# Other places for the first five and the last four of 32 elements in a hand-ordered decoder kernel, and ten fewer filler products

## The chip, the cores and the metric

The kernel runs on one core of a Trainium2 chip. Its time is the device time in microseconds (us) of that core, from the first to the last instruction and what lies around them. It holds one launch with 32 independent batch elements. The engines are TensorE (PE), VectorE (DVE), ScalarE (ACT), GpSimd (POOL) and SyncE (SP, which here only issues DMAs).

## The reference

Four layers are applied to `x` (32 elements of 128 tokens by 256 features) with a context of the same shape. Cut to what matters:

```
# layer 0: attention of x with the context; only element 0's result is used, and is added to all
return tgt + att[0]
# layer 1: a Mamba block, then cross attention with 8 heads
zxbcdt = rms(x, norm_w) @ in_proj_w;  z, xBC, dt = split(zxbcdt);  dt = softplus(dt + dt_bias)
xBC = silu(conv_b + sum(padded[:, k:k+L] * conv_w[:, k] for k in range(4)))
h = h * exp(dt * A) + (dt * xh) B^T;  y = h C            # a scan over the 128 tokens, 8 heads
x = x + rms((y + D_skip * xh) * silu(z)) @ out_proj_w
x = x + softmax(masked(ln(x) Wq (enc Wk)^T / sqrt(dh))) (enc Wv) @ Wo
# layer 2: causal self attention, layernorm, cross attention, layernorm, relu feed-forward, layernorm
# layer 3: causal cross attention, layernorm, gelu feed-forward (256 -> 1024 -> 256), residual
```

## The kernel before

An element passes through some 93 tasks, each with a name: `x1` (x plus layer 0's result), `x1r` and `xhat` (its normalised input), `xhatT`, `z0`, `z1`, `xbc0`, `xbc1` (input projections), `dt`, `softplus`, `am`, `ld` (the step widths and the decay rates, a long chain of small operations on POOL), `spread` (the rates sent to all 128 partitions through DRAM), `conv0`, `conv1`, `silu`, `pairs`, `scan`, `decayed`, `Y` (the Mamba block), `uT`, `proj`, `xnT`, `Q1`, `K1`, `V1`, `quads1`, `scores1`, `turn1`, `values1`, `finish1`, `ctxT`, `Wo` (the first attention) and so on to `up0`, `up1`, `down`, `store`. The attentions 2, 3 and 4 have `quads` (scores), `mT` (row maxima turned), `quadsT` (scores turned), `exps`, `values`, `attT`, `back`, `finish` and `norm`. `x1.1` below is task `x1` of element 1, the second one; elements are counted from 0. One task can have parts on several engines: `V4` is a product on PE, an addition on DVE and a memset on POOL.

The order of the tasks on every engine is fixed when the kernel is built. Each task has a due time in `TASKS`; element n stands 14 units after element n-1. The first eight elements are moved by the numbers in `FIRST`, the last six by those in `LAST`, tasks that are done once stand at `SETUP`, and `SHIFT` moves a task on one engine against PE:

```
moved = FIRST.get(task, ...)[n] if n < FEW_FIRST else LAST.get(task, ...)[n - B] if n >= B - FEW_LAST else 0
return round(TASKS[task] + PERIOD * n + moved, 4)
```

Every engine then runs its tasks strictly in that order, and waits at each for what it needs. So does the queue of SP: a transfer is issued only when all that stand before it have been. The results of products go to four PSUM banks that are used in turn (`job`, L282): a product waits until the job four places before it in PE's order has been read out.

In places where PE is expected to wait, `spare` (L630) has it multiply the identity matrix with itself a given number of times; the results are never read. `SPARE` gives the counts for the start (113 in all), `SPARE_LAST` those for the last element (36):

```
for _ in range(times):
    mm(t[:, 0:P], ident, ident, start=True, stop=True)
```

The loads of all weights are issued at the start by SP in the order `load_mamba`, `load_w1`, `load_w2`, and then `loadx.1`, the input of element 1. `load_w3` (five transfers, 2.75 MB) comes later. `x1` needs its element's input to have landed:

```
dve.wait_ge(S[f"x_in{l % 2}"], nth_of_two(it, l) * 16)
```

Of the kernel before, what the change touches and what calls it, by code (L numbers as in the profile page):

```python
# [54 lines left out]
    finish2=43.1974, finish3=49.378, finish4=63.2585, ld=21.3616, loadc=21.5812, loadx=-12.121, mT2=40.0837, mT3=48.4859,
    mT4=58.9877, n2=40.7882, n3=47.7104, norm2=33.7236, norm3=22.9718, norm4=37.5768, norm5=62.8256, pairs=21.8762, proj=26.9634,
    quads1=31.0824, quads2=38.3064, quads3=46.4563, quads4=57.4583, quadsT2=40.7773, quadsT3=49.6848, quadsT4=61.9224, row=44.5976,
    scan=14.2492, scores1=32.2004, scores2=32.0011, scores3=47.3368, scores4=68.1586, silu=20.9204, softplus=18.9875,
# [1647 lines left out]
```

## Time and profile before

| what | us |
|---|---|
| median of 3 runs (1661.57 to 1665.08) | 1662.71 |
| the profiled execution | 1660.65 |
| its span, first to last instruction | 1658.9 |
| PE busy in it | 1610.9 |
| DVE busy in it | 1387.6 |
| ACT busy in it | 1075.2 |
| POOL busy in it | 499.7 |

The profile is of one execution, 2.06 us shorter than the median. Busy times include the filler products. A row of the timeline gives the start in us from the span's start, the busy time, engine, line, operation, what is written and read, the shapes and the count; in brackets the idle time just before it and what ended it. A float32 product of the program is two records on PE, so 9 filler products are x18 there.

### The profile page before, as it was taken

To read this page: it belongs to the slowest core of one execution; us is meant where nothing else is said; L and a number is where in the kernel's file an instruction comes from. 1 tells how busy PE (TensorE), PEld (TensorE's weight loads), DVE (VectorE), ACT (ScalarE), POOL (GpSimd) and SP (SyncE) were. 2 spreads that over 40 slices of the span, in tenths; PEclk is the share of its full clock that TensorE was granted. 3 is DMA by queue.
4 is the path that set the end of the run, shared out by engine and by line. 5 is a ranking of instruction groups with operands and counts; after the bars stand their busy time and mean duration, and the time that the engine had idled before them with its cause. 6 is when DMAs were issued, how large, how long until landed. Compare 5 with 4: busy or idle time off the path is not lost.

```text
span 1658.9 us, 61223 instructions
## 1 busy us (share of the span) xinstructions
PE 1610.9 (97%) x25035; PEld 1386.5 (84%) x25035; DVE 1387.6 (84%) x3587; ACT 1075.2 (65%) x2798; POOL 499.7 (30%) x1256
## 2 busy tenths in 40 slices
PE   7899999999999999999999999999999999999987
PEld 6778888888888888888888888888888888888776
DVE  4688888888888889888889888888988888898662
ACT  2356766776666676666667676667766666766663
POOL 2333223333322332332233232233333223323110
PEclk9999999999999999999999999999999999999999
DMA  6210001000000000000000000000000000000000
GB/s 224 76 36 24 3 18 31 18 24 28 22 3 24 25 25 25 25 23 4 25 25 25 25 25 7 20 24 25 25 25 25 2 25 25 22 28 19 5 5 8
DMA packets 31317, 44.38 MB, mean 27 GB/s; under 512 B 3008, under 2 KB 26176, under 8 KB 30912
## 3 DMA queue, kind: packets, MB, share of 16 engines
q1 hardware_dynamic: 30496, 39.93, 7.6%
q8 instruction: 202, 3.31, 0.9%
q14 instruction: 75, 0.61, 0.1%
q10 hardware_dynamic: 544, 0.52, 0.1%
HBM read 36.12 MB, written 4.33 MB: 24 GB/s over the span
## 4 chain that ended last, share of the span: by engine, by line
PE 54%; DVE 36%; issue 4%; POOL 3%; DMA 1%; ACT 1%; DVEq 0%; SPq 0%; POOLq 0%; ACTq 0%
PE ring L639 19%; PE ring L645 14%; PE ring L627 5%; DVE conv L1371 5%; DVE maxima_at L1269 5%; PE score L707 4%; DVE decay L1405 4%; PE score L731 2%; PE ring L773 2%; DVE conv L1377 2%; DVE decay L1409 2%; PE ring L860 2%; DVE QB L1280 2%; DVE bn L1239 2%; DVE conv L1366 2%
## 5 line engine op out<-in xcount | busy, mean ns | idle before, releaser
L1546 POOL TENSOR_TENSOR stat<-stat 128x1 f32<-128x1 f32 x224 | 132.0, 596 | 603.3 <-DVE stat L1235 602.8
L1026 ACT COPY actT<-ring 128x256 f32<-128x256 f32 x256 | 95.6, 374 | 259.0 <-PE ring L627 258.7
L1269 DVE TENSOR_REDUCE maxima_at<-score 128x4 f32<-128x512 f32 x388 | 240.8, 684 | 21.0 <-PE score L707 19.8
L1059 ACT ACTIVATE weights<-score 128x512 f32<-128x512 f32 x388 | 200.6, 606 | 28.1 <-PE score L731 27.6
L1371 DVE SCALAR_TENSOR_TENSOR conv<-raw,vectors,conv 128x128 f32<-128x128 f32 x576 | 168.5, 348 | 6.8
L639 PE MATMUL ring<-actT,w_q 128*128 128x128 f32 x1024 | 141.5, 281 | 0.7 <-ACT actT L1026 0.7
L639 PEld LDWEIGHTS ring<-actT,w_q 128*128 128x128 f32 x1024 | 124.5, 191 | 12.8 <-issue 11.3
L639 PE MATMUL ring<-actT,w_up 128*128 128x128 f32 x1024 | 127.6, 278 | 0.5 <-ACT actT L1026 0.5
L639 PEld LDWEIGHTS ring<-actT,w_up 128*128 128x128 f32 x1024 | 119.1, 192 | 3.5 <-ACT actT L1026 1.0
L1195 ACT ACTIVATE gT<-ring,vectors 128x128 f32<-128x128 f32 x256 | 73.2, 369 | 68.7 <-PE ring L639 68.0
L645 PE MATMUL ring<-w_down,gT 128*128 128x256 f32 x512 | 115.9, 379 | 1.3 <-issue 1.3
L731 PE MATMUL score<-QB,KE 32*128 32x128 f32 x3104 | 114.8, 284 | 1.0 <-DVE QB L1280 1.0
L731 PEld LDWEIGHTS score<-QB,KE 32*128 32x128 f32 x3104 | 96.2, 187 | 19.9 <-issue 15.4
L773 PE MATMUL ring<-weights,V 128*32 128x128 f32 x3104 | 104.9, 276 | 1.6 <-issue 1.3
L1077 ACT ACTIVATE KE<-K,const 128x128 f32<-128x128 f32 x256 | 106.3, 503 | 0.0
L645 PEld LDWEIGHTS ring<-w_down,gT 128*128 128x128 f32 x512 | 94.9, 190 | 13.1 <-issue 1.4
L639 PE MATMUL ring<-cT,w_k 128*128 128x128 f32 x768 | 104.4, 279 | 0.0
L1070 ACT COPY attT<-ring 128x512 f32<-128x512 f32 x97 | 56.3, 580 | 71.0 <-PE ring L773 70.8
L645 PE MATMUL ring<-w_v,cT 128*128 128x256 f32 x384 | 100.6, 385 | 0.5 <-ACT V L1043 0.5
L639 PEld LDWEIGHTS ring<-cT,w_k 128*128 128x128 f32 x768 | 95.4, 192 | 4.9 <-issue 0.2
L1280 DVE SCALAR_TENSOR_TENSOR QB<-ring,const,QB 128x256 f32<-128x256 f32 x194 | 84.4, 476 | 17.7 <-PE ring L627 17.6
L773 PEld LDWEIGHTS ring<-weights,V 128*32 128x32 f32 x3104 | 79.1, 109 | 23.5 <-ACT V L1043 11.8
(180 smaller groups left out, 3843.9 us busy)
## 6 DMA issues: line engine op xcount, KB each, us to landing
decay<-rates_out SPq DMA_DIRECT2D x32, 512.0 KB, 4.1
cT<-in_ctxT SPq DMA_DIRECT2D x32, 128.0 KB, 2.2
x_in<-in_x SPq DMA_DIRECT2D x32, 128.0 KB, 2.5
out<-result SPq DMA_DIRECT2D x32, 128.0 KB, 2.1
row_all<-in_rows SPq DMA_DIRECT2D x1, 1420.0 KB, 10.2
w_in<-in_in_proj SPq DMA_DIRECT2D x1, 1288.0 KB, 6.9
w_k<-in_k SPq DMA_DIRECT2D x4, 256.0 KB, 8.6
w_v<-in_v SPq DMA_DIRECT2D x4, 256.0 KB, 7.6
```

The lines of the kernel that those rows point to most:

```text
L627: last = nc.tensor.transpose(t[:, c * P:(c + 1) * P], src[:, c * P:(c + 1) * P], ident)
L639: last = mm(t[:, at:at + P], w[:, c, cols:cols + P], xT[:, c, :], start=(c == 0), stop=(c == n - 1))
L645: last = mm(t[:, at:at + hi - lo], xT[:, c, :], w[:, c, lo:hi], start=(c == 0), stop=(c == n - 1))
L731: last = mm(score[:, r, at:at + P], KE[rows_of, l, c, e, :], QB[rows_of, l, c, e, :], start=(not masked and at == 0), stop=(c == DC - 1 an ...
L773: last = mm(output[ROWS_OF[r], four * P:(four + 1) * P], V2[:, l, h, :], weights[:, buffer, h % 8 // 2, at:at + P], start=True, stop=True)
L1026: nc.scalar.copy(dst.rearrange("p c k -> p (c k)"), t[:, 0:n]).then_inc(read, 1)
L1059: run(weights[:, turned_buffer(it, a_, l), r, :], score[:, r, :], ACT.Exp).then_inc(S["exps"], 1)
L1077: last = run(KE[:, l, c, e, :], K2[:, l, c, :], ACT.Identity, scale=own[:, e:e + 1], bias=spare_row[:, 2 * c + e:2 * c + e + 1])
L1269: nc.vector.tensor_reduce(maxima_at[:, maxima_buffer(it, a_, l), 32 * r:32 * (r + 1)].rearrange("p (f s) -> p s f", f=2)[:, 0:DC, :], scor ...
L1280: last = stt(QB[:, l, :, e, :], t[:, 0:P].unsqueeze(1).broadcast_to((P, DC, P)), either_row[:, e:e + 1], QB[:, l, :, e, :], ALU.mult, ALU.add)
L1371: last = stt(conv[:, l % 2, c, :], raw[:, l % 2, c, k:k + P], conv_w[:, c, k:k + 1], conv[:, l % 2, c, :], ALU.mult, ALU.add)
L1546: tt(stat[:, l, 10:11], stat[:, l, 2:3], stat[:, l, 4:5], ALU.pow).then_inc(S[done], 1)
```

## The change

`TASKS`, `SHIFT` and `SPARE_LAST` have the same numbers as before. New are the entries of elements 0 to 4 in `FIRST` and of elements 28 to 31 in `LAST` (all 93 tasks of each), all of `SETUP`, and 9 of the 15 counts in `SPARE`. No instruction is added or taken away but filler products: 103 in place of 113. Elements 5 to 27 keep their due times, and PE runs the same order as before from `fc2.5` to `values1.25`. Two of the changed table lines, and the counts:

```
-    x1=(-5.3355, -6.7716, -12.2611, 0.5214, 0.2413, 0.0991, 0, 0.8625),
+    x1=(-5.017, -12.3112, -7.2487, 0.1142, 1.8596, 0.0991, 0, 0.8625),
...
-SPARE = {("mT0", 0): 11, ("values0", 0): 9, ("back0", 0): 3, ("xhatT", 0): 6, ("ld", 0): 16, ("pairs", 0): 5, ("Y", 0): 18, ("uT", 0): 6, ("xnT", 0): 9, ("ctxT", 0): 10, ("x2T", 0): 7, ("Y", 1): 3, ("mT2", 0): 4, ("back2", 0): 3, ("n3", 0): 3}
+SPARE = {("mT0", 0): 11, ("values0", 0): 9, ("back0", 0): 3, ("xhatT", 0): 13, ("ld", 0): 16, ("pairs", 0): 5, ("Y", 0): 14, ("uT", 0): 6, ("xnT", 0): 6, ("ctxT", 0): 7, ("x2T", 0): 4, ("Y", 1): 2, ("mT2", 0): 3, ("back2", 0): 3, ("n3", 0): 1}
```

The new tables stand on more lines, so every line behind them has a number that is higher by 22.

**DVE, around the first use of element 1's input.** Before, behind element 0's normalised input (`att<-res,stat`) come the preparations of constants, `q1_bias` to `k4_bias` and on to the weights, and only after both convolutions `res<-x_in,att0`, which is `x1.1`:

```order
L1307 TENSOR_SCALAR att<-res,stat 128x256
L1333 TENSOR_SCALAR q1_bias<-ring2 128x1
L1333 TENSOR_SCALAR q1_bias<-ring3 128x1
...
L1371 SCALAR_TENSOR_TENSOR conv<-raw,vectors,conv 128x128 x9
L1299 TENSOR_TENSOR res<-x_in,att0 128x256
L1377 SCALAR_TENSOR_TENSOR conv<-raw,conv 128x768
L1393 TENSOR_TENSOR state_gate<-ring3,const 128x128
L1397 TENSOR_TENSOR dbx<-ring0,dts 128x512
L1399 TENSOR_TENSOR dx<-ring0,row_all 128x512
L1235 TENSOR_SCALAR stat<-stat 128x1
L1405 SCALAR_TENSOR_TENSOR decay<-decay,delta 128x1024
```

Of the change, from the same instruction on (L1329 is the L1307 above):

```order
L1329 TENSOR_SCALAR att<-res,stat 128x256
L1321 TENSOR_TENSOR res<-x_in,att0 128x256
L1355 TENSOR_SCALAR q1_bias<-ring3 128x1
L1355 TENSOR_SCALAR q1_bias<-ring0 128x1
...
L1399 SCALAR_TENSOR_TENSOR conv<-raw,conv 128x768
L1374 TENSOR_SCALAR w_q1<-w_q1,vectors 128x256 x2
L1329 TENSOR_SCALAR att<-res,stat 128x256
L1415 TENSOR_TENSOR state_gate<-ring3,const 128x128
L1419 TENSOR_TENSOR dbx<-ring0,dts 128x512
L1421 TENSOR_TENSOR dx<-ring0,row_all 128x512
L1427 SCALAR_TENSOR_TENSOR decay<-decay,delta 128x1024
```

`x1.1` moved from behind the convolutions to the place ahead of the preparations, and `xhat.1` (the second L1329) stands ahead of element 0's `pairs` and `scan`; before it stood behind element 0's `xnT`.

**SP, from the first `spread` on.** `decay<-rates_out` is `spread`, `rates_out<-rates_row` is `ld`; the five rows from `w_q` to `w_down` are `load_w3`. Before:

```order
L582 DMA decay<-rates_out 128x1024
L578 DMA rates_out<-rates_row 8x128
L573 DMA cT<-in_ctxT 128x2x128
L561 DMA x_in<-in_x 128x256
L582 DMA decay<-rates_out 128x1024
L555 DMA w_q<-in_q 128x2x256
L555 DMA w_k<-in_k 128x2x256
L555 DMA w_v<-in_v 128x2x256
L555 DMA w_up<-in_up 128x2x1024
L555 DMA w_down<-in_down 128x8x256
```

Of the change:

```order
L604 DMA decay<-rates_out 128x1024
L577 DMA w_q<-in_q 128x2x256
L577 DMA w_k<-in_k 128x2x256
L577 DMA w_v<-in_v 128x2x256
L577 DMA w_up<-in_up 128x2x1024
L577 DMA w_down<-in_down 128x8x256
L600 DMA rates_out<-rates_row 8x128
L595 DMA cT<-in_ctxT 128x2x128
L604 DMA decay<-rates_out 128x1024
```

`load_w3` follows element 0's `spread` directly; before it followed element 1's.

**PE, the last element's last attention.** `w_v4,cT` is `V4.31`, `w_fc2` is `fc2.31`, `QB,KE` is `quadsT4.31`, `ring2<-const` are nine filler products, `weights,V2` is `values4.31`. Before:

```order
L639 MATMUL ring3<-actT,w_fc1 128x128 x4
L645 MATMUL ring0<-w_v4,cT 128x256 x2
L645 MATMUL ring1<-w_fc2,fc1T 128x256 x2
...
L731 MATMUL score<-QB,KE 128x128 x16
L634 MATMUL ring2<-const 128x128 x9
L773 MATMUL ring2<-weights,V2 32x128 x16
```

Of the change:

```order
L661 MATMUL ring3<-actT,w_fc1 128x128 x4
L667 MATMUL ring0<-w_fc2,fc1T 128x256 x2
...
L753 MATMUL score<-QB,KE 128x128 x16
L667 MATMUL ring1<-w_v4,cT 128x256 x2
L656 MATMUL ring2<-const 128x128 x9
L795 MATMUL ring2<-weights,V2 32x128 x16
```

`V4.31` moved from between `fc1.31` and `fc2.31` to the place between `quadsT4.31` and the fillers.

## Rows read from the trace of the kernel before

**Rows 1.** The page's first part: busy us, share of the span, instructions
```profile
PE 1610.9 (97%) x25035; PEld 1386.5 (84%) x25035; DVE 1387.6 (84%) x3587; ACT 1075.2 (65%) x2798; POOL 499.7 (30%) x1256
```

**Rows 2.** Windows: stretch, length, busy us by engine, granted TensorE clock, DMA share, GB/s
```profile
0.00:80.00 80.00, 64.35 (x681) 57.52 (x685) 44.40 (x125) 24.88 (x70) 24.63 (x62) 0.98 0.43 141
80.00:160.00 80.00, 74.17 (x1235) 61.14 (x1234) 69.68 (x182) 47.30 (x126) 27.36 (x70) 1.00 0.13 41
160.00:1540.00 1380.00, 1369.54 (x21746) 1182.52 (x21739) 1214.78 (x3132) 942.36 (x2459) 433.87 (x1096) 1.00 0.07 21
1600.00:1660.00 60.00, 47.55 (x547) 40.10 (x547) 19.83 (x50) 23.24 (x53) 5.13 (x11) 0.93 0.02 6
```

**Rows 3.** Timeline of DVE, element 0: `xhat`, the last preparation, `softplus`
```profile
24.05 0.35 DVE L1307 TENSOR_SCALAR att<-res,stat 128x256 f32<-128x256 f32 x1 [0.85 <-POOL stat L1546]
...
26.01 0.45 DVE L1342 TENSOR_SCALAR k_bias<-vectors,const 128x1 f32<-128x1 f32 x2
...
29.32 0.17 DVE L1385 TENSOR_SCALAR dts<-dts 128x8 f32<-128x8 f32 x1 [1.28 <-ACT dts L1110]
```

**Rows 4.** The line that loads inputs (L561), 21 to 23 us: `loadx.1`
```profile
L561 SPq DMA_DIRECT2D x_in<-in_x x1: 1077/1077/1077, 21.8 to 21.8; - x1
...
DMA to landing us min/median/max: 7.1/7.1/7.1
```

**Rows 5.** Timelines of POOL (`softplus.0` begins) and PE (`ld.0`)
```profile
30.11 0.20 POOL L1571 TENSOR_TENSOR dts<-dts 128x8 f32<-128x8 f32 x1 [1.06 <-DVE dts L1387]
...
36.15 0.27 PE L851 MATMUL ring<-const,dts 128*8 128x128 f32 x1 [3.37 <-POOL dts L1591]
```

**Rows 6.** The line of `spread` (L582), for element 0 and element 1
```profile
L582 SPq DMA_DIRECT2D decay<-rates_out x1: 430/430/430, 38.1 to 38.1; - x1
DMA to landing us min/median/max: 4.0/4.0/4.0
...
L582 SPq DMA_DIRECT2D decay<-rates_out x1: 430/430/430, 73.0 to 73.0; - x1
...
DMA to landing us min/median/max: 5.2/5.2/5.2
```

**Rows 7.** Timeline: both scans, element 0's first attention, element 1's chain between them
```profile
42.94 2.28 DVE L1405 TENSOR_TENSOR_SCAN decay<-decay,delta 128x1024 f32<-128x1024 f32 x1
...
59.84 1.29 DVE L1260 TENSOR_REDUCE neg_max<-score 128x4 f32<-128x512 f32 x2 [3.67 <-PE score L687]
...
64.99 0.17 DVE L1387 TENSOR_TENSOR dts<-dts 128x8 f32<-128x8 f32 x1
65.54 0.76 PE L750 MATMUL ring<-V,weights 128*32 128x33 f32 x64 [1.04 <-ACT weights L1064]
...
65.96 2.70 DVE L1371 SCALAR_TENSOR_TENSOR conv<-raw,vectors,conv 128x128 f32<-128x128 f32 x9
...
68.82 0.42 DVE L1440 TENSOR_TENSOR att<-ring,rec 128x256 f32<-128x256 f32 x1
...
71.08 0.27 PE L851 MATMUL ring<-const,dts 128*8 128x128 f32 x1 [0.48 <-POOL dts L1591]
...
78.18 2.29 DVE L1405 TENSOR_TENSOR_SCAN decay<-decay,delta 128x1024 f32<-128x1024 f32 x1 [1.04 <-DMA decay<-rates_out]
```

**Rows 8.** Timeline of DVE: `xnT.1`
```profile
92.08 0.41 DVE L1245 TENSOR_SCALAR att<-res,stat 128x256 f32<-128x256 f32 x1 [0.77 <-POOL stat L1546]
```

**Rows 9.** Timelines of the tail: `scores3.30`, `V4.31`, nine fillers, `values4.31`
```profile
1561.84 2.49 DVE L1269 TENSOR_REDUCE maxima_at<-score 128x4 f32<-128x512 f32 x4 [2.49 <-PE score L707]
...
1621.00 1.03 PE L645 MATMUL ring<-w_v,cT 128*128 128x256 f32 x4
...
1638.10 2.27 PE L634 MATMUL ring<-const 128*128 128x128 f32 x18
1640.35 1.08 PE L773 MATMUL ring<-weights,V 128*32 128x128 f32 x32
```

**Rows 10.** Windows with PE alone: stretch, length, busy, granted clock, DMA
```profile
38.00:40.00 2.00, 2.00 (x9) 0.50 0.79 238
```

More of the change, by code:

```diff
@@ L55 @@
[L55 to L58, printed above, removed]
@@ new lines @@
+    pairs=21.8762, proj=26.9634, quads1=31.0824, quads2=38.3064, quads3=46.4563, quads4=57.4583, quadsT2=40.7773,
+    quadsT3=49.6848, quadsT4=61.9224, row=44.5976, scan=14.2492, scores1=32.2004, scores2=32.0011, scores3=47.3368,
+    scores4=68.1586, silu=20.9204, softplus=18.9875, spread=22.7901, store=23.1605, turn1=32.8102, uT=26.5226, up0=66.8312,
+    up1=67.8745, values1=33.4323, values2=42.004, values3=50.5514, values4=63.0522, x1=14.4949, x1r=12.6782, x2T=35.2831,
+    x3T=44.7168, x4T=52.7176, x5T=55.6828, x6T=65.7536, xbc0=16.7051, xbc1=18.0605, xhat=30.6529, xhatT=15.884, xnT=28.5927,
@@ L194 @@
-        fc1=0.7372, ld=-0.1039, row=0.2044, scores1=-0.7902, silu=-0.1882, softplus=-0.2365, turn1=0.1793, uT=0.4762, up0=0.6797,
-        up1=0.4246, x1=-0.5175, x2T=-0.0673, x3T=0.071, x4T=0.2522, x5T=0.318, x6T=0.3578, xbc0=0.1868, xbc1=0.439, xhatT=0.0635,
-        xnT=0.9282, z0=0.0015, z1=0.2322, K0=-24.9607, Q0=-31.7526, V0=-0.7018, attT0=-21.6729, exps0=39.9731, prep_in=-3.1006),
-    DVE=dict(
-        K1=1.0572, K3=0.57, V4=0.4841, Wo=1.1062, Y=0.609, conv0=3.1201, conv1=22.4343, decayed=-7.3402, down=1.5737, e2=0.5677,
-        e3=-0.0785, fc2=0.652, finish1=43.3665, finish2=0.278, finish3=2.0689, finish4=1.3234, mT2=0.6229, mT3=0.8259, mT4=0.5286,
-        n2=0.9079, n3=0.7485, norm2=10.4211, norm3=29.708, norm4=17.8864, norm5=2.0685, pairs=0.2116, proj=0.8909, scan=10.8396,
-        scores1=-0.5025, scores2=7.84, scores3=-0.7238, scores4=-9.0893, silu=1.0136, softplus=0.4775, uT=0.6437, x1=-1.3524,
-        x1r=1.7364, x3T=0.0339, xhat=-15.2978, xnT=0.2024, finish0=3.4964, mT0=-11.4439, prep_in=10.1597, prep_masks=14.7529,
-        prep_out=12.705, prep_q1=-0.1445, scores0=-43.4431),
+        K0=-24.9607, K2=0.4275, K4=0.371, KE2=2.1051, KE3=-8.3627, Q0=-31.7526, Q1=0.2401, Q2=0.4113, Q3=0.0246, Q4=1.2096,
@@ new lines @@
+        V0=-0.7018, V1=0.0661, V2=0.6553, V3=0.3112, Y=1.0681, attT0=-21.6729, attT2=-3.4331, attT3=31.0217, attT4=8.7138,
+        ctxT=-0.4571, exps0=39.9731, exps2=-6.4438, exps3=39.9244, exps4=40.2808, fc1=0.7372, ld=-0.1039, prep_in=-3.1006,
+        row=0.2044, scores1=-0.7902, silu=-0.1882, softplus=-0.2365, turn1=0.1793, uT=0.4762, up0=0.6797, up1=0.4246,
+        x1=-0.5175, x2T=-0.0673, x3T=0.071, x4T=0.2522, x5T=0.318, x6T=0.3578, xbc0=0.1868, xbc1=0.439, xhatT=0.0635,
+        xnT=0.9282, z0=0.0015, z1=0.2322),
@@ new lines @@
+    DVE=dict(
+        K1=1.0572, K3=0.57, V4=0.4841, Wo=1.1062, Y=0.609, conv0=3.1201, conv1=22.4343, decayed=-7.3402, down=1.5737,
+        e2=0.5677, e3=-0.0785, fc2=0.652, finish0=3.4964, finish1=43.3665, finish2=0.278, finish3=2.0689, finish4=1.3234,
+        mT0=-11.4439, mT2=0.6229, mT3=0.8259, mT4=0.5286, n2=0.9079, n3=0.7485, norm2=10.4211, norm3=29.708, norm4=17.8864,
+        norm5=2.0685, pairs=0.2116, prep_in=10.1597, prep_masks=14.7529, prep_out=12.705, prep_q1=-0.1445, proj=0.8909,
+        scan=10.8396, scores0=-43.4431, scores1=-0.5025, scores2=7.84, scores3=-0.7238, scores4=-9.0893, silu=1.0136,
+        softplus=0.4775, uT=0.6437, x1=-1.3524, x1r=1.7364, x3T=0.0339, xhat=-15.2978, xnT=0.2024),
```

280 lines of the change are left out of this document (149 added, 131 removed).

## The prediction

> **What bounds the kernel now.** I read the busy times first, then the windows. PE is busy for 1610.9 of 1658.9 us [rows 1], so it is the engine to look at; but the windows split the kernel in three [rows 2]. From 160 to 1540 us PE is busy 1369.54 of 1380 us: the middle is PE's own work, and no order of tasks can shorten it by more than the 10.5 us left. In the first 80 us PE is busy 64.35 and DVE 44.40: neither is full, so chains of single operations set the pace there, and much of PE's time is filler: the counts up to `x2T.0` are 100 of the 113. From 80 to 160 us PE is busy 74.17 and DVE 69.68; both are near their limit. In the last 60 us PE is busy 47.55, DVE 19.83: chains again. So the change, which touches the ends alone, can win only what its chains become shorter at the two ends; once PE is full, a shift is handed on unchanged through the middle to the tail, since the same work follows.
>
> Then I read the timelines of both ends for what ended each wait. In the start one chain stands out for each element: the step widths on POOL, `ld` on PE, `spread` by DMA, the scan on DVE. Element 0's scan begins at 42.94, element 1's at 78.18, and the second is released by the DMA [rows 7]. What moves that 78.18 moves what follows.
>
> **The change part by part.**
>
> *Ten fewer fillers.* Nine take 2.27 us [rows 9], so ten are 2.5 us. They cost something only where PE would otherwise be ready earlier; at all the places where the counts fall, PE waits for DVE or ACT behind the fillers anyway. Priced at nothing; what covers it is that wait. Without it the gain would be up to 2.5 us.
>
> *x1.1 ahead of the preparations.* Element 1's input is issued at 21.8 behind all weights and lands 7.1 us later, at 28.9 [rows 4]. DVE is free for it when `xhat.0` ends, 24.05 + 0.35 = 24.40 [rows 3]. DVE takes its tasks in order, so it stands for 4.5 us, and behind it wait the preparations (24.40 to 26.01 + 0.45 = 26.46, 2.1 us [rows 3]) and `softplus.0`. `x1.1` itself has no row here; as a pass over 256 elements like `xhat.0` it is taken as 0.4. `softplus.0` on DVE then begins at 28.9 + 0.4 + 2.1 = 31.4, not 29.32 [rows 3]: 2.1 us late. The move of the weight scalings behind the convolutions doesn't help, since DVE had waited 1.28 before that anyway. PE is touched too: `bias0` now lies in the bank that `xbc1.0` needs, and is read by the first preparation, so `xbc1.0` waits till 29.5; `conv1.0` needs it only at 35, so that costs nothing.
>
> From the start of `softplus.0` on POOL (30.11) to `ld.0` (36.15) are 6.0 us of fixed steps [rows 5], so `ld.0` goes to 38.3. `spread.0` was issued at 38.1 and goes to 40.2. It took 4.0 us, but now `load_w3` is issued right behind it, as it was behind element 1's, and that one took 5.2 [rows 6]. So the rates land at 45.4 with the 5.2, at 44.2 with the 4.0. I take 5.2: it is the row with the same five transfers behind it. The scan of element 0 goes from 42.94 to 45.4, 2.5 us late (bounds 1.3 and 2.5).
>
> Two transfers on one queue start in order, says the Trainium skill (DMA: Bandwidth & Descriptors, Two DMAs through the same engine are not ordered), but are pipelined. By order alone `load_w3` behind could not slow `spread`, the 4.0 would hold, and the sum below would be 1.2 us lower. The 5.2 of element 1 speaks against it, with one row.
>
> *xhat.1 ahead of the first scan.* Element 1's projections now fill PE beside element 0's scan, and its `conv0` stands on DVE ahead of `scores1.0`, where DVE waited 3.67 us [rows 7]; it took 3.5 us there (2.70 in nine passes and 0.85 in three, as `conv1.1` [rows 7]), and fits. `scores1.0` itself follows element 0: 59.84 + 2.5 = 62.3. Behind it, with no convolution between, comes `softplus.1`: 1.3 for the maxima and 0.6 for three small steps give 64.2, where before they ended at 64.99 + 0.17 = 65.16 [rows 7]. That is 1.0 us earlier. The same POOL chain then releases `ld.1` at 71.08 - 1.0 = 70.1; before, it had ended a 0.48 us wait of PE [rows 7], so it was the last. In its way on PE stands `ctxT.0`, which needs `finish1.0`; that had waited for `conv1.1` until 68.8, and now stands ahead of it. `values1.0` ended at 65.54 + 0.76 = 66.30 [rows 7], 6.5 us behind the start of `scores1.0`; in that, ACT did the copies of `z1.1`, `xbc1.1` and `V1.1` between the exponentials and the turned weights, about 1.6 us that the new order puts elsewhere. So `finish1.0` comes at 62.3 + 4.9 = 67.2. `spread.1` goes from 73.0 to 72.0, and, with no `load_w3` behind, takes 4.0 instead of 5.2: it lands at 76.0. Element 1's scan goes from 78.18 to 76.0: **2.2 us earlier**. With `spread.0` at 4.0 as well it would be 3.4. The other way to the scan, `conv1.1` from 67.8 (3.5), its tanh and product (0.9 and 1.0) and `pairs.1` (1.9), ends at about 75.8, just in time. So the late element 0 is forgiven, as long as nothing there takes longer.
>
> *xhat.2 ahead of xnT.1.* It fills 0.35 of a wait of 0.77 on DVE [rows 8] in a stretch where DVE is near full: 0.35 us. Other exchanges between 80 and 500 us have no row of their own; bounded by PE's idle time, (80 - 74.17) in 80 to 160 and about 2 behind it, and below by the same on the other side. I take nothing.
>
> *The tail.* `quads1.31` waited for its bank; `Q3.30` (a product of about 1 us) now stands in that place, and `turn1.31` and its wait no longer stand ahead of `quads3.30`. `scores3.30`, for which DVE waited 2.49 from 1559.35 [rows 9], can begin as soon as some 1560.4 instead of 1561.84, and everything of element 31 up to `Wo` follows it by 1.2 us. Against it, `V4.31` took 1.03 where PE waited for ACT's relu in any case, and now stands in front of nine fillers whose end (1640.37) met the start of `values4.31` at 1640.35 [rows 9]: there was no room, so it costs 1.0. Net -0.2.
>
> Sum: -2.2 - 0.35 - 1.2 + 1.0 = -2.7 us. Against the profiled 1660.65 that is 1657.9. That execution lies 2.06 below the median of 1662.71; moved to the median, **1660.0**.
>
> **The clock.** After PE's wait of 3.37 before `ld.0` [rows 5] the granted clock fell to half, 0.50 in 38 to 40 us [rows 10], which is the 1.2 GHz level; there nine records filled 2 us. In the change PE waits twice, 1.3 before `xbc1.0` and some 2.4 before `ld.0`. If it falls again, V1.0 and five fillers stand twice as long ahead of `pairs.0`, some 1.2 us more; that is inside the wait for the rates. In the tail the clock is 0.93 over the last 60 us [rows 2]; a stretch more or less at half clock moves the end by 1 to 2 us either way.
>
> The Trainium skill (TensorE: Matmul & The Clock Gate, What's actually happening) has activity release the throttle. By that rule fewer fillers are a risk, not a gain: each stretch that falls costs as said above, a sum up to 1.5 us higher. The row after `ld.0`'s wait agrees; no row shows it after a wait under 1 us.
>
> **The rivals.**
> *More is won* (0.34). `spread.0` isn't slowed by `load_w3` (-1.2), PE isn't at half clock near `pairs.0`, and the fuller DVE order of elements 1 to 4 saves a part of the 5.8 us of PE's idle time in 80 to 160 us, some 1.5: 1660.0 - 2.7 = 1657.3. For it: both stretches are near full, so each wait filled counts. Against: DVE, not PE, has the longer queue there.
> *Nothing arrives* (0.16). Element 1's scan comes 2.2 earlier, but PE spends it waiting later, before element 3; the tail is -0.2. 1662.5. For it: the last scans of the start are already at the steady distance. Against: from 92 us on DVE has hardly a wait to lose it in.
> *Slower, the wait for element 1's input* (0.12). The 4.5 us of DVE at `x1.1` aren't forgiven: `finish1.0` now stands ahead of `conv1.1`, and with 75.8 against 76.0 there is no slack. If element 0's attention or `conv1.1` comes later than here worked out, each us goes through. It decides from 2.2 us on; above that, the whole delay of element 0 and the loss of that gain show. An input that lands 4 us later than 28.9, with the queue as full as it is, gives -2.7 + 2.2 + 4 = +3.5: 1666.2.
>
> **How the numbers follow.** My forecast has 0.38, with its own range 1658.4 to 1661.6 (bounds of `spread` and one half-clock stretch). A measurement of this kernel tells 0.2%, 3.3 us, from no change, so faster is below 1659.4. Of the forecast a third lies below, with the first rival 0.34: 0.45. The second rival and the rest of the forecast: 0.42. Slower than 1666.0: 0.13. The range holds the forecast, nearly all of the first two rivals: 1655.2 to 1663.8.
>
> **What would show it.** In the changed kernel DVE waits 4.5 us for the DMA at `x1.1` (L1321) from 24.4; `ld.0` at 38.3; scans at 45.4 and 76.0; `spread.0` 5.2 and `spread.1` 4.0 us to landing; `finish1.0` ahead of `conv1.1` near 67; the middle as far apart as before; in the tail `V4.31` directly before the fillers and `values4.31` at 1.0 more behind `quadsT4.31`. The forecast is wrong if element 1's scan isn't near 76, or if the distance from it to the first full stretch grows.

## The result and the profile after

The change is slower, not faster: 1665.54 us median of 20 executions against 1662.53 of the kernel before, ratio 1.0022, 95% interval 1.0014 to 1.0031. In three later comparisons it stood 8.1, 6.9 and 5.9 us above the kernel before. The forecast was 1660.0, or 2.7 faster.

The page's first part for the changed kernel (compare [rows 1]), and its windows, in the columns of [rows 2]:

```profile
PE 1611.0 (97%) x25015; PEld 1387.0 (83%) x25015; DVE 1391.1 (84%) x3587; ACT 1075.3 (65%) x2798; POOL 494.6 (30%) x1256
```

```profile
0.00:80.00 80.00, 63.31 (x677) 56.98 (x677) 48.43 (x125) 25.71 (x70) 23.00 (x61) 0.96 0.48 161
80.00:160.00 80.00, 72.83 (x1208) 60.03 (x1212) 69.54 (x182) 47.07 (x126) 26.44 (x71) 1.00 0.06 16
160.00:1540.00 1380.00, 1366.42 (x21680) 1180.05 (x21674) 1211.23 (x3126) 941.11 (x2456) 431.49 (x1096) 1.00 0.07 21
```

The third row is the surprise. PE works there at the same full clock, and from 336 to 1363 us it has the same products in the same order as before; still it is busy 1366.42 of 1380 us where it was 1369.54, so it is idle 3.1 us more in a stretch of which the change touches only the two ends. The profiled execution took 1667.32 us, 6.7 more than that of before. When each product of PE is held against the same product of the kernel before, the changed kernel is level at 370 us (0.02 late), 2.3 late at 1363 us and 6.7 late at the end. So about a third of this execution's loss lies in the untouched middle, and two thirds behind it.

The first 80 us went nearly as worked out. DVE's timeline, with `x1.1`'s wait, `softplus.0`'s last step on DVE and both scans (compare [rows 3] and [rows 7]):

```profile
28.51 0.42 DVE L1321 TENSOR_TENSOR res<-x_in,att 128x256 f32<-128x256 f32 x1 [4.42 <-DMA x_in<-in_x]
...
31.35 0.17 DVE L1409 TENSOR_TENSOR dts<-dts 128x8 f32<-128x8 f32 x1
...
45.06 2.28 DVE L1427 TENSOR_TENSOR_SCAN decay<-decay,delta 128x1024 f32<-128x1024 f32 x1
...
67.56 0.42 DVE L1462 TENSOR_TENSOR att<-ring,rec 128x256 f32<-128x256 f32 x1
...
75.72 2.28 DVE L1427 TENSOR_TENSOR_SCAN decay<-decay,delta 128x1024 f32<-128x1024 f32 x1
```

And `ld.0` on PE, then the line of `spread` for elements 0 and 1 (compare [rows 5, 6]):

```profile
37.73 0.27 PE L873 MATMUL ring<-const,dts 128*8 128x128 f32 x1 [2.57 <-POOL dts L1613]
```

```profile
L604 SPq DMA_DIRECT2D decay<-rates_out x1: 430/430/430, 39.7 to 39.7; - x1
DMA to landing us min/median/max: 5.2/5.2/5.2
...
L604 SPq DMA_DIRECT2D decay<-rates_out x1: 339/339/339, 71.4 to 71.4; - x1
DMA to landing us min/median/max: 3.6/3.6/3.6
```

DVE stands 4.42 us for the input (forecast 4.5), `ld.0` is at 37.73 (38.3), the first `spread` takes 5.2 (5.2), the scans begin at 45.06 (45.4) and 75.72 (76.0). So the second scan is 2.5 us earlier than before, and the step on it was right. It was worth little all the same, and what was lost came later.

**Where the middle lost.** Timelines of PE over element 8's `quadsT4` (`score<-QB,KE`, 32 records of products): the kernel before; the changed one, with its next long stops; and another profile of the changed one (`change_third` below):

```profile
540.18 1.17 PE L731 MATMUL score<-QB,KE 32*128 32x128 f32 x32
```

```profile
540.18 0.94 PE L753 MATMUL score<-QB,KE 32*128 32x128 f32 x21
542.28 0.71 PE L753 MATMUL score<-QB,KE 32*128 32x128 f32 x11 [1.17 <-issue]
...
1275.55 0.50 PE L753 MATMUL score<-QB,KE 32*128 32x128 f32 x8 [1.39 <-issue]
...
1569.47 0.18 PE L940 MATMUL ring<-nonzero,ones_bf 128*128 128x16 bf16 x1 [1.46 <-issue]
```

```profile
541.57 0.71 PE L753 MATMUL score<-QB,KE 32*128 32x128 f32 x11 [1.45 <-issue]
```

PE stops in the middle of a run of equal products whose operands have long been there, after 21 of 32, for over a microsecond, and no engine released it ("issue" is a wait for nothing that the profile shows). The other profile of the change stops after the same 21. With a third one of 0.48 us at 1520 us the stops make 3.04 us, which is the 3.1 of the windows. The next stop of that kind stands at the start of the tail, and there the granted clock falls behind it as well (1570 to 1580 us, same columns as above):

```profile
1570.00:1575.00 5.00, 4.13 (x43) 2.63 (x46) 1.88 (x5) 2.34 (x5) 0.83 (x2) 0.63 0.02 3
1575.00:1580.00 5.00, 4.96 (x76) 4.38 (x76) 1.86 (x7) 3.76 (x8) 0.00 (x0) 0.68 0.00 0
```

**What the stops coincide with.** The page's part on DMA queues (packets, MB, share) has a queue q8 that no line of the kernel uses, for the kernel before and for the changed one:

```profile
q8 instruction: 202, 3.31, 0.9%
```

```profile
q8 instruction: 201, 3.29, 0.8%
```

3.31 MB in 202 packets are 16 KB each. PE has 2 x 25035 = 50,070 records before [rows 1] and 50,030 after: one packet for 248 records. So q8 brings PE's program, in pieces, while it runs. (The page has a second queue of this kind, q14, with 75 packets of 8 KB; nothing here rests on it.) The Trainium skill (Perfetto Trace Analysis, The 4-stage abstract model) has instructions of 64 bytes; by it, as an estimate, a packet is 256 instructions. The trace agrees: with PE's semaphore instructions, which the page's counts leave out, the kernel before has 51,669 records, or 201.8 times 256. The forty records fewer are the ten fillers: a float32 product is two products and two weight loads. So the middle has moved against the borders of the pieces, by 40 instructions with fewer fillers alone, and by 37 in the change, where PE has three semaphore instructions more. What q8 did from 529 to 539.5 us, ahead of the stop, in the kernel before, and all packets there in the changed one:

```profile
q8 instruction: 1, 0.02, 0.5%
```

```profile
DMA packets 0, 0.00 MB, mean 0 GB/s; under 512 B 0, under 2 KB 0, under 8 KB 0
```

The piece that the kernel before had fetched by then (at 536.65) is asked for only at 539.90 in the changed one, 12.2 us behind the one ahead of it (527.74) and in the midst of dense products, of which `values1` and `quadsT4` use 64 records in about 1 us each. PE stops 1.2 us after the request (the packet takes 0.99) and goes on at 542.28, which is 2.4 after it.

**PE stops at the borders of the pieces.** That can be read from the traces directly. Count all of PE's records in the trace, weight loads, products and semaphore instructions. In the change PE goes on at record 16,321 (counted from 0), which is 63 x 256 + 193. In `fewer_fillers` (below) it stops after 23 of the 32 products and not after 21, and that is record 16,321 again, since the three semaphore instructions are missing:

```profile
542.82 0.59 PE L731 MATMUL score<-QB,KE 32*128 32x128 f32 x9 [1.18 <-issue]
```

All 27 stops of over 0.9 us (24 in the table below and the 3 of the change's first profile), in 13 profiles of nine kernels with different orders and counts, end at such a place: 193 or 194 behind a multiple of 256, and 2.2 to 2.9 us after q8 began a packet. What sets them apart is how far ahead of the border the request comes. Between 160 and 1600 us the 20 profiles have 3642 requests. In 27 of them PE was 82 instructions or fewer ahead of the border, and it stopped each time (26 times over 0.9 us, once 0.5). The others came 85 or more ahead, and only one of them has a stop over 0.9 us (at 86). The latest of all is in `before_20_more`, where PE was at the border when the request came, and it has the longest stop:

```profile
1565.30 0.40 PE L677 MATMUL score<-causal_bf,ident_bf 32*32 32x512 bf16 x6 [1.96 <-issue]
```

In the change's profile the request for piece 63 came 43 instructions ahead.

### The profile page after: what moved, and what is told of

It reads as the page before. It is cut to its first block, busy times and chain, and to the rows that moved or that the text cites. A ratio compares the mean times of both kernels' runs of the same rounds, so it can differ in the third digit from the quotient of the medians.

```text
span 1665.5 us, 61187 instructions
## 1 busy us (share of the span) xinstructions
PE 1611.0 (97%) x25015; PEld 1387.0 (83%) x25015; DVE 1391.1 (84%) x3587; ACT 1075.3 (65%) x2798; POOL 494.6 (30%) x1256
## 4 chain that ended last, share of the span: by engine, by line
PE 62%; DVE 30%; issue 4%; POOL 2%; SPq 1%; ACT 1%; DMA 0%; DVEq 0%; POOLq 0%; ACTq 0%
PE ring L661 20%; PE ring L667 16%; PE ring L649 7%; DVE conv L1393 5%; PE score L729 5%; DVE maxima_at L1291 4%; PE score L753 4%; PE ring L795 3%; DVE decay L1427 3%; PE ring L882 2%; PE score L693 2%; DVE decay L1431 2%; DVE conv L1399 1%; DVE conv L1388 1%; DVE bn L1261 1%
```

## The experiments

Medians in us of the kernel and of the kernel before in the same comparison, ratio with its 95% interval, and how many waits of over 0.9 us PE has between 160 and 1575 us of the profiled execution that are marked as issue. All 18 lie within 2% of the kernel before; what is read from them are differences of a few us.

| kernel | median | before | ratio | stops |
|---|---|---|---|---|
| `start_alone` (= the change) | 1668.31 | 1660.23 | 1.0045 (1.0032 to 1.0059) | 4 |
| `tail_alone` | 1660.27 | 1660.23 | 0.9998 (0.9990 to 1.0007) | 0 |
| `fewer_fillers` | 1667.35 | 1660.23 | 1.0037 (1.0022 to 1.0051) | 4 |
| `tail_v4_back` | 1659.21 | 1660.23 | 0.9992 (0.9982 to 1.0001) | 0 |
| `counts_back_in_step` | 1663.08 | 1660.98 | 1.0015 (0.9999 to 1.0031) | 1 |
| `change_back_in_step` | 1660.66 | 1660.98 | 0.9998 (0.9986 to 1.0010) | 1 |
| `before_out_of_step` | 1664.04 | 1660.98 | 1.0016 (1.0003 to 1.0028) | 1 |
| `change_again` | 1667.83 | 1660.98 | 1.0035 (1.0018 to 1.0052) | 4 |
| `start_in_step` (= the change, 20 tiny) | 1661.07 | 1659.56 | 1.0009 (1.0000 to 1.0017) | 2 |
| `change_v4_back` | 1660.31 | 1659.56 | 1.0002 (0.9993 to 1.0010) | 1 |
| `before_20_more` | 1662.17 | 1659.56 | 1.0019 (1.0010 to 1.0028) | 1 |
| `change_x1_later` | 1658.21 | 1659.56 | 0.9993 (0.9984 to 1.0001) | 0 |
| `start_only_in_step` | 1661.99 | 1662.63 | 0.9993 (0.9978 to 1.0008) | 0 |
| `best_of_both` | 1657.93 | 1662.63 | 0.9970 (0.9957 to 0.9984) | 1 |
| `change_148_more` | 1664.34 | 1662.63 | 1.0011 (0.9996 to 1.0025) | 1 |
| `change_ten_fillers` | 1661.31 | 1662.63 | 0.9993 (0.9979 to 1.0007) | 0 |
| `change_third` | 1666.16 | 1660.22 | 1.0030 (1.0019 to 1.0042) | 3 |
| `best_ten_fillers` | 1658.59 | 1660.22 | 0.9982 (0.9971 to 0.9993) | 0 |

The change's first profile has 3 such stops, that of the kernel before none.

**Which part costs.** In the first four kernels parts of the new tables are put into the kernel before: in `start_alone` `FIRST`, `SETUP` and `SPARE` (and `LAST`, see below), in `tail_alone` `LAST`, in `fewer_fillers` `SPARE` (8 of its 15 counts differ, not 9: seven fillers more ahead of `xhatT.0`, seventeen fewer at seven places), in `tail_v4_back` `LAST` with one number changed:

```diff
-    V4=(-0.3497, 0.201, -0.2438, 0.7662, 4.9017, 101.7904),
+    V4=(-0.3497, 0.201, -0.2438, 0.7662, 4.9017, 5.8734),
```

> The new order of elements 0 to 4, the new numbers of the work done once and the new filler counts, with the old order of elements 28 to 31. Theory A, the tail is what costs: the start's gain at scan.1 (2.5 us earlier in the trace) is gone by element 3, so this kernel stands within 0.5 us of the one before and at least 2 us below the full change. Theory B, the start costs: PE's waits there are longer and it stands 2 to 3.5 us above the one before. Theory C, neither: the 3 us of the full change come from pauses that hit any execution, and this one is within 1 us of both.

> The old order up to element 27 and the new order of elements 28 to 31 alone. Theory A: 2.5 to 4 us above the kernel before, nearly all of the full change's 3.0. Theory B: within 0.5 us of it, or 0.2 below as forecast. The profile should show under A the same late place as the full change: quads3.30 waiting for the exponentials of element 31's first attention, ctxT.31 behind n3.30, and a stretch at half clock near 60 us before the end of element 29's values.

> The old order everywhere with the new filler counts (seven more ahead of xhatT.0, seventeen fewer at eight places behind it). If the fillers' time is covered by PE's waits, 0 within 0.5 us. If the waits behind the shorter fillers let the clock fall, 0.5 to 1.5 us slower; if the fillers had stood in the way, up to 2.5 us faster.

> As the new tail alone, but with the last product of values' input of element 31, V4.31, back where it stood, between fc1.31 and fc2.31. If its place costs what was forecast, 1.0 us below the new tail alone. If the nine fillers and ScalarE's exponentials leave room for it, no difference within 0.4 us; then the tail's loss is elsewhere, between 1555 and 1580 us.

`start_alone` held the new `LAST` as well, against its description; it is the full change once more, at +8.1. The new tail is worth 0.0, so theory A fell. The surprise is `fewer_fillers`: the old order everywhere and ten fillers fewer is 7.1 us slower, as much as the whole change. `V4.31` costs 1.06 us by the medians (1660.27 against 1659.21); with twelve executions of each, the 95% interval is -0.6 to 1.8, and the traces of the two kernels have 0.8 (4.54 against 3.72 us from `quadsT4.31`'s first record to `values4.31`), where 1.0 was forecast.

**Place in the blocks, or the waits around the fillers?** `tick` adds products of 32x32 on 16 columns, two records each, that take next to no time:

```diff
+            def tick(it, what, lane, times):
+                t, full = claim(it, what, lane)
+                for _ in range(times):
+                    mm(t[0:32, 0:16], ident_bf[0:32, 0:32], ident_bf[0:32, 0:16], start=True, stop=True)
...
+                    if i == 0 and (task, l) == ("ld", 0):
+                        tick(Of(i), RING_JOBS.get(task, task).split()[0], l, 20)
```

Twenty of them are 40 records, as many as the ten fillers that are gone. "In step" means below that PE's records of the middle have their old numbers again. Theory D has the stops come from the place in the blocks, theory E from the waits around the shorter fillers. `counts_back_in_step` is that in `fewer_fillers`, `change_back_in_step` in the change, `before_out_of_step` in the kernel before with 108 in place of 20.

> The old order with the new filler counts, and 20 tiny products (32x32 on 16 columns, bf16, results never read) in PE's wait ahead of ld.0. Ten fillers are 40 records on PE (20 products, 20 weight loads); 20 tiny products are 40 records too, so from there on every instruction of the middle has the same number in PE's program as in the kernel before. Theory D, PE's code arrives in blocks of 256 instructions (16 KB), and the 40 fewer instructions moved the block borders to places where dense products follow and PE stands 1.2 us: then this kernel is back at the time before, within 1 us, about 7 below the fewer fillers alone. Theory E, the shorter filler runs let PE wait and its clock fall, or shift the start: then it stays 5 to 7 us above the one before. The profile under D has no stop of over 1 us near 543, 1031 and 1276 us.

> The full change with the same 20 tiny products ahead of ld.0. Theory D: the stops in the middle (542 and 1275 us, 1.2 and 1.4 us) and the one at 1569 us (1.5 us) go; 2.5 to 5 us below the full change, so at or below the kernel before, and what is left is the worth of the new order alone (forecast -2.7). Theory E: within 1 us of the full change.

> The kernel before, all fillers kept, with 108 tiny products ahead of ld.0: 216 more records, which is 40 fewer in steps of 256. They take some 1 to 2 us in a wait of 3.4 us, so in themselves nothing. Theory D: 4 to 8 us slower than the kernel before, with stops at the same elements (8, 13, 18, 23, 28) as with fewer fillers. Theory E: within 1 us of the kernel before.

> The full change once more, on the same chip as the three others: 2 to 4 us above the kernel before if chips agree. The stops should stand at the same records of PE (15803, 38878 and 48060 of its program) as in the first profile if code is their cause, and elsewhere or nowhere if they are chance.

Twenty products that compute nothing make the change 7.2 us faster (1667.83 to 1660.66 in one comparison), though PE has more to do (95% interval 4.1 to 8.6). With the fewer counts in the old order they take +7.1 down to +2.1. And 108 of them make the kernel before 3.1 slower, with a stop of 1.46 us at 542.93, within the same `quadsT4` of element 8. Theory E fell for the bulk; D's number for `counts_back_in_step` (within 1 us) was missed, and so were its 4 to 8 us for `before_out_of_step`. `change_again` at +6.9 missed its 2 to 4. The profiles say why: in step, the stops at the old records are gone, but some stand elsewhere (at 737 us in `counts_back_in_step`, at 493 in `change_back_in_step`, both within `quadsT4` products).

**The same with one edit more.** `start_in_step` is `start_alone` with 20 tiny products and so again the full change in step; `change_v4_back` has the line of `V4` above; `before_20_more` is the kernel before with 20 tiny products; in `change_x1_later`:

```diff
-    x1=(-5.017, -12.3112, -7.2487, 0.1142, 1.8596, 0.0991, 0, 0.8625),
+    x1=(-5.017, -6.7716, -7.2487, 0.1142, 1.8596, 0.0991, 0, 0.8625),
```

> The new order and counts of elements 0 to 4 with the old tail, and the 20 tiny products ahead of ld.0, so that PE's instructions from the middle on have the numbers of the kernel before. The same start without them stood 8.1 us above the kernel before. The prediction's own working gives -2.5 here. Theory D and the traces so far (the shift at element 7 was -1.0 to +1.1 in five profiles): 0 to -1.5 us. If it stays 3 or more us above, code blocks are not what made the new start slow.

> The full change with the 20 tiny products, and V4.31 back between fc1.31 and fc2.31. Its place cost 1.06 us between the two kernels with the old start, near the forecast of 1.0. So 1 us below the change with the tiny products alone, at 1659 to 1660 where the kernel before stands at 1660.5 to 1661: the fastest of all so far, if by less than a measurement tells.

> The kernel before with 20 tiny products ahead of ld.0: 40 records more in front of the middle, in a wait of 3.4 us, so in themselves nothing. Theory D: the block borders move by 40 the other way. If only one sort of place is bad, this is as fast as before, within 1 us; if the old numbering is the lucky one, 2 to 5 us slower with stops of 1.2 us at other records. Rival theory: any added product ahead of ld.0 disturbs the start, which should show as a shift by element 2 already.

> The full change with the 20 tiny products, and x1.1 alone back behind the convolutions of element 0, so that DVE no longer stands for element 1's input at 24 us. The prediction's working: element 0's scan begins 2.1 us earlier than in the change (43.5), but element 1's scan hardly moves since the delay of element 0 was forgiven; so 0 to -0.5 us. If the delay was not forgiven, 1 to 2 us below the change with the tiny products.

The change in step stood at -0.3 and +1.5: two measurements of one thing, 1.8 apart. `change_v4_back` at +0.75 shows nothing beyond that, and it isn't the fastest of all, as was expected. `before_20_more` is 2.6 slower: adding records harms as removing does, so the old numbering was among the good ones. `change_x1_later` is 1.35 below the kernel before (its interval just includes no change) and without a stop. Its two scans on DVE, the wait for the input gone:

```profile
42.06 2.28 DVE L1435 TENSOR_TENSOR_SCAN decay<-decay,delta 128x1024 f32<-128x1024 f32 x1
...
73.42 2.28 DVE L1435 TENSOR_TENSOR_SCAN decay<-decay,delta 128x1024 f32<-128x1024 f32 x1
```

Element 0's scan is 3.0 us earlier than in the change and element 1's 2.3 (75.72 to 73.42). So the delay by `x1.1` was not forgiven at the second scan, against what the prediction had.

**What counts, and a version without the two costs.** `start_only_in_step` has the new tables but the old `LAST`, and 20 tiny products; `best_of_both` is the change with 20 tiny products and both edits, `x1` and `V4`; `change_148_more` has 148 tiny products; `change_ten_fillers` none, but

```diff
-("ld", 0): 16
+("ld", 0): 26
```

> The two kernels called start above turned out to hold the new order of elements 28 to 31 as well, so they are the full change again, without and with the 20 tiny products. This one is what they were meant to be: new order and counts of elements 0 to 4, old order of the last four, 20 tiny products ahead of ld.0. The change with the tiny products stood at -0.3 and +1.5 in two comparisons, the new tail alone at 0.0. So theory D gives -0.5 to +1.5 here; the prediction's own working gives -2.5. If it is below -1.5 the start's gain had been there and the new tail had eaten it.

> The change with the tiny products, x1.1 behind the convolutions and V4.31 back between fc1.31 and fc2.31. x1.1 alone gave -1.35 against the kernel before, V4.31 -1.06 beside the old start. So 1.4 to 2.4 us below the kernel before: faster than both kernels, by 0.1%.

> The full change with 148 tiny products ahead of ld.0 in place of 20: 296 records more than the change, which is 40 more in steps of 256, so the block borders of the middle fall on the same records as with 20. If the place within a block of 256 is what counts, it stands with the 20 (-0.3 to +1.5 against the kernel before) and 5 or more below the change. If it is the local effect of a few products ahead of ld.0, or the whole number of instructions, it can stand anywhere. It may add up to 1 us of its own, since 148 fill the whole wait.

> The full change with ten ordinary identity products more ahead of ld.0 (26 in place of 16), so 113 in all as in the kernel before, 40 records more. No tiny products, so nothing that is new to the kernel. Theory D: as with the 20 tiny products, -0.3 to +1.5 against the kernel before. They also take 2.5 us of a wait of some 2.6 us ahead of ld.0, so PE may reach ld.0 up to 0.3 late. If it stays at +3 to +8, it is not the count.

> The full change, beside the best version on one chip. It stood 3.0, 8.1 and 6.9 us above the kernel before in three comparisons; the kernel before was at 1662.5, 1660.2 and 1661.0 in them. So 3 to 8 us above it, with the stop at PE's record 15803 again.

> The change with x1.1 behind the convolutions, V4.31 back between fc1.31 and fc2.31, and ten ordinary fillers more ahead of ld.0 (113 in all): the best version without tiny products. Theory D: as the one with tiny products, 1.5 to 4.7 us below the kernel before, and 6 to 10 below the change on the same chip. The rival, that chance decides: within 2 us of the change.

Ten ordinary fillers put back in another place do what the tiny products did: -1.3 against the kernel before, where the change is +3.0 to +8.1. PE over element 8's `quadsT4` in it, with the 32 records in one piece again:

```profile
540.72 1.17 PE L753 MATMUL score<-QB,KE 32*128 32x128 f32 x32
```

The records of PE's program at which the pieces 61 to 64 of q8 were asked for, counted in each trace:

| kernel | 61 | 62 | 63 | 64 |
|---|---|---|---|---|
| before | 15084 | 15266 | 15578 | 15869 |
| `change_ten_fillers` | 15084 | 15266 | 15582 | 15852 |
| the change | 15162 | 15322 | 15760 | 15914 |
| `change_third` | 15162 | 15322 | 15768 | 15924 |

In step, the requests fall on nearly the records of before, though the order of the start differs; out of step, piece 63 is asked for some 180 records later, just as `quadsT4` of element 8 begins, and PE stops at record 15803 (16,321 with the semaphore instructions).

`change_148_more` is +1.7, just outside what was expected. Its 148 products delay element 0's scan (47.13, against 44.86 to 45.76 with 20 and the same order of `x1.1`), some 2 us of its own, so in the rest it stands with the kernels in step, and its stop at 497 us is at PE's record 14572, 256 behind that of `change_back_in_step` at 14316: the place within a block of 256 is what stayed the same. The new start alone, in step, stands at -0.6, with an interval from -3.7 to +1.3 us.

Both edits on top give -4.7 with tiny products, more than the 1.4 to 2.4 expected, and -1.6 (0.9982, 0.9971 to 0.9993) with ordinary ones, the latter 7.6 below the change in the same comparison. The two stand at 1657.93 and 1658.59 themselves; most of what parts them is the kernel before, at 1662.63 in one comparison and 1660.22 in the other. `best_ten_fillers` is the best kernel here without products that are new to it: the change with ten fillers at `ld.0`, `x1.1` behind the convolutions and `V4.31` ahead of `fc2.31`. PE's middle (160 to 1540 us, columns of [rows 2]) is whole again, 1369.42 us busy against 1369.54 before:

```profile
160.00:1540.00 1380.00, 1369.42 (x21740) 1183.54 (x21741) 1214.29 (x3133) 943.01 (x2462) 431.99 (x1096) 1.00 0.07 21
```

## Why the prediction was wrong

**The step that failed** is the first one, "ten fewer fillers": "Priced at nothing; what covers it is that wait." It priced the fillers by their time alone. By their number they cost 7.1 us in the old order (`fewer_fillers`), and putting the number back takes 7.2 off the change. With it fell "once PE is full, a shift is handed on unchanged through the middle": in the changed kernel the middle added 3.0 us of stops, and the tail's beginning one more of 1.46. In the four profiles of the change the stops between 370 and 1363 us sum to 2.6, 4.0, 3.7 and 2.6 us (first profile, `start_alone`, `change_again`, `change_third`), and PE falls behind the kernel before by 2.3, 3.8, 5.1 and 2.3 there. None of the rivals had this. The slower rival (1666.2) gave nearly the right time, but its mechanism didn't occur: the input landed as forecast, at 28.5, and the second scan was not late.

**Element 0 and the two scans**: right within 0.6 us for the wait, `ld.0` and both scans. But "the late element 0 is forgiven" was wrong: without the wait the second scan comes 2.3 us earlier. What that is worth in time is known less well. The kernel is 1.05 us better by one pair (-1.35 against -0.3, each beside the kernel before) and 2.9 better by the other, within one comparison (1658.21 against 1661.07 of `start_in_step`); but the profile of `change_x1_later` has no stop, and those of the two others one and two.

**The start's gain** (-2.2 and -0.35 forecast): -0.6 alone, in step (`start_only_in_step`), but its interval includes the forecast. The traces say more: in the change's first profile the second scan is 2.5 us earlier than before, and at 370 us PE is level with the kernel before (0.02 late; 1.2 late, 1.0 and 1.0 early in the three others). The mechanism of the second rival was right here: PE spends the gain waiting ahead of element 3. PE's waits from 105 to 123 us, changed kernel and then before (`res` is `x2T.1`, `conv` is `pairs.2`):

```profile
110.54 0.41 PE L649 MATMUL ring<-const,res 128*128 128x128 f32 x2 [0.90 <-issue]
112.17 0.49 PE L867 MATMUL ring<-conv 128*128 128x128 f32 x2 [1.22 <-DVE conv L1399]
120.66 0.31 PE L933 MATMUL ring<-q_first,K 128*32 128x8 f32 x16 [0.90 <-POOL q_first L1619]
```

```profile
109.74 1.13 PE L645 MATMUL ring<-w_v,cT 128*128 128x256 f32 x4 [0.49 <-ACT V L1043]
...
122.65 0.44 PE L627 MATMUL ring<-const,res 128*128 128x128 f32 x2 [0.92 <-DVE res L1252]
```

The longest waits make 3.0 us against 1.4. From 80 to 160 us PE is busy 72.83 where it was 74.17 [rows 2]. A part of it is an overlap that moved. GpSimd's two passes of `z0.2` now lie beside `conv1.2` on DVE; before they lay beside the scan. POOL and DVE, changed and before:

```profile
106.96 1.65 POOL L1607 TENSOR_SCALAR tz<-tz 128x512 f32<-128x512 f32 x1
108.69 1.27 POOL L1608 TENSOR_TENSOR zs<-tz,zs 128x512 f32<-128x512 f32 x1
```

```profile
105.98 4.13 DVE L1393 SCALAR_TENSOR_TENSOR conv<-raw,vectors,conv 128x128 f32<-128x128 f32 x9
```

```profile
114.88 1.27 POOL L1586 TENSOR_TENSOR zs<-tz,zs 128x512 f32<-128x512 f32 x1
```

```profile
106.94 2.70 DVE L1371 SCALAR_TENSOR_TENSOR conv<-raw,vectors,conv 128x128 f32<-128x128 f32 x9
...
114.91 3.39 DVE L1405 TENSOR_TENSOR_SCAN decay<-decay,delta 128x1024 f32<-128x1024 f32 x1 [0.21 <-DMA decay<-rates_out]
```

The nine passes take 4.13 in place of 2.70, and the scan 2.28 where before it took 3.39: the operations of DVE that meet the two passes on POOL are held by 1.1 to 1.4 in all. Ahead of `Wo.1` and `silu.2`, for which PE waits, that costs. That it costs there was read from the rows, not tried alone.

**The tail** (-0.2 forecast): 0.0 measured, and of its two terms the +1.0 of `V4.31` is 1.06 by medians and 0.8 in the trace. The other, -1.2, was not tried alone; `tail_v4_back`, the new tail without the first term, stands at -1.0 with an interval that just includes no change. From the first record of `quadsT4.31` to `values4.31` are 4.54 us in the changed kernel, 3.72 before [rows 9]:

```profile
1642.46 0.44 PE L693 MATMUL score<-causal_bf,ident_bf 32*32 32x512 bf16 x16 [0.97 <-DVE QB L1302]
...
1643.93 1.13 PE L667 MATMUL ring<-w_v,cT 128*128 128x256 f32 x4
1644.90 2.17 PE L656 MATMUL ring<-const 128*128 128x128 f32 x18
1647.00 1.08 PE L795 MATMUL ring<-weights,V 128*32 128x128 f32 x32
```

**The spread behind load_w3**: 5.2 was taken against 4.0, and 5.2 it was; the second took 3.6. In the 20 profiles the one with `load_w3` behind it took 4.3 to 6.1 us and the other 3.3 to 4.2, so what is queued behind does slow it. It didn't decide: DVE came to the first scan straight from `pairs.0`, with no wait.

**The clock**: 0.96 in place of 0.98 over the first 80 us, and 0.69 where it had been 0.50 at 38 to 40 us [rows 10]. The rule that fewer fillers risk the clock did not make the loss: from 160 to 1540 us both kernels ran at 1.00. But a stop can take the clock with it, and then costs more than itself. In `change_again` it fell behind the stop that ended at 541.51 us (stretch, length, busy, granted clock, DMA); that is the profile above in which PE lost 5.1 us over stops of 3.7:

```profile
543.00:546.00 3.00, 3.00 (x9) 0.50 0.00 0
```

Behind the stop at 1569 us it fell in two of the change's four profiles. From 1363 us to the end these two lost 4.4 us each, the other two 0.4 and 1.4.

**What stays open.** That PE stops for want of its next piece is shown; what makes the request late is not. In step, some stops moved to other records, and executions of one kernel scatter: the change's first 20 lie between 1661.72 and 1669.91, those of the kernel before between 1659.26 and 1668.91. Stops are not all of that scatter: the profiled execution of `start_only_in_step` took 1665.16 us without one of over 0.9. So a numbering is not good or bad for certain, only likely so. The loss of the change also differed between comparisons, 3.0 to 8.1, which one profile each doesn't explain.

## What to carry to other kernels

On a full engine with a long unrolled program, an edit that only adds or removes a few instructions renumbers all that follow, and can cost or give more than its own time: before an order is judged, bring the instruction count back to what it was, with fillers where the engine waits anyway. Look for stops inside a run of equal instructions, marked as issue, at the same record in two profiles; they are not the order's doing. To be sure, count all records of the engine up to the place where each stop ends: here all of them ended at the same place within 256. Only then do steps of 1 us, such as a wait for an input moved forward or a product put where no wait covers it, show what they are worth.

## What the runs showed of the hardware that was not expected

- PE's program comes in packets of 16 KB by a DMA queue of its own during the execution: 202 packets for 50,070 records. When the next one is asked for late PE stops, at the border of the pieces and for up to 1.96 us, in the middle of products that are ready: each time when the request came 82 instructions or fewer ahead of the border, in 27 of 3642 cases. One page of the Trainium skill (Trainium Architecture — The Big Picture, The software stack) has the instruction streams sent to the engines when the program is loaded; this trace shows them coming while it runs.
- The change's stops in the middle stand in a grid of about 245 us, five elements of 48.9 us (542, 788 and, two steps on, 1277 us in `change_again`), within `quadsT4` of elements 8, 13 and 23.
- Twenty products of 32x32 on 16 columns, results unused, took 7.2 us off a kernel of 1668.
- Beside a GpSimd product of 128x512 (1.27 us) a DVE pass that takes 0.35 us alone took 1.42, and a scan of 2.28 took 3.39.
